# A relational graph layer on one core: ScalarE's order within a block, stores in four pieces, a bank for the totals, dense comparisons

## What is computed

```
h = relu(layernorm(x))                                   # (6250, 128)
dots   = sum((h[src] @ tokeys.T) * relations[rel] * (h[src] @ toqueries.T), axis=1) / 128
values = exp(dots)
fr     = src + 6250 * rel
values = values / segment_sum(values, fr)[fr]
output = segment_sum(values[:, None] * h[dst], fr)       # (16 * 6250, 128)
weights = einsum('rb,bij->rij', comps, bases_w)          # 16 matrices of 128 x 128
out = relu(einsum('rij,rnj->ni', weights, output))
return x + out
```

## Time and profile before

| | |
|---|---|
| median of 3 runs | 2487.49 us (2487.05 to 2491.51) |
| profiled execution, its own time | 2487.54 us |
| its span, first to last instruction | 2485.8 us (1.7 us lie around it) |
| PE busy | 1327.6 us, 53% of the span |
| DVE busy | 1336.7 us, 54% |
| ACT busy | 454.1 us, 18% |
| POOL busy | 1613.0 us, 65% |
| mean granted TensorE clock | 0.723 |

### The profile page before, as it was taken

How to read it: one execution, slowest core, us unless ns; L and a number is a source line. 1 busy time by engine, 2 the same in 40 slices (tenths; PEclk the granted TensorE clock), 3 DMA queues, 4 the chain that set the end, 5 groups by cost and what they waited for, 6 DMA issues and landing times.

```text
span 2485.8 us, 30053 instructions
## 1 busy us (share of the span) xinstructions
PE 1327.6 (53%) x9063; PEld 1000.5 (40%) x9113; DVE 1336.7 (54%) x2311; ACT 454.1 (18%) x868; POOL 1613.0 (65%) x1828
## 2 busy tenths in 40 slices
PE   2888988345453535454454545463545454454443
PEld 2665666234242424334342434342434344343433
DVE  7888888474545454454545454545454444545450
ACT  3555555210101011111101010101011111111010
POOL 3122222377777777777777777777777777777775
PEclk8999999666666767676666666666767676666666
DMA  4333333122222222222222222222222222222222
GB/s 124 139 139 127 134 139 137 53 54 56 54 56 54 55 54 56 54 55 54 56 55 54 56 54 56 54 56 54 56 54 56 54 56 54 55 54 56 55 54 41
DMA packets 77959, 170.30 MB, mean 69 GB/s; under 512 B 29796, under 2 KB 45148, under 8 KB 71511
## 3 DMA queue, kind: packets, MB, share of 16 engines
q0 software_dynamic: 52576, 106.12, 17.1%
q1 hardware_dynamic: 25010, 63.79, 7.0%
q10 hardware_dynamic: 352, 0.14, 0.0%
HBM read 112.99 MB, written 57.82 MB: 69 GB/s over the span
## 4 chain that ended last, share of the span: by engine, by line
POOL 59%; issue 21%; PE 15%; DMA 2%; DVE 1%; POOLq 1%; ACT 1%; SPq 0%; ACTq 0%; DVEq 0%
POOL arena L456 59%; PE bank L1112 7%; PE bank L1097 3%; PE bank L1065 1%; ACT H L907 1%; POOLq L448 1%; DMA bucket_streams<-REC,IDXW 1%; PE bank L1087 1%; PE bank L1104 1%; PE bank L1078 0%; DMA stage<-in_edge_type 0%; PE bank L1105 0%; PE bank L1225 0%; DVE stats L555 0%; PE bank L1123 0%
## 5 line engine op out<-in xcount | busy, mean ns | idle before, releaser
L456 POOL DMA_INDIRECT arena<-Z_messages,IDX x1593 | 1504.0, 944 | 495.3 <-issue 485.1
L1225 PE MATMUL bank<-arena 128*128 128x128 f32 x3528 | 514.7, 320 | 747.0 <-DMA arena<-Z_messages,IDX 747.0
L1225 PEld LDWEIGHTS bank<-arena 128*128 128x128 f32 x3528 | 506.8, 235 | 757.3 <-issue 757.3
L763 DVE SCALAR_TENSOR_TENSOR O<-bank,X 128x128 f32<-128x128 f32 x49 | 14.3, 292 | 725.4 <-PE bank L1225 725.4
L1015 ACT COPY pay_all<-bank 128x1024 bf16<-128x1024 bf16 x147 | 108.0, 807 | 1368.1 <-PE bank L1192 1359.5
L755 DVE TENSOR_TENSOR arena<-stage,bank 128x512 f32<-128x512 bf16 x441 | 267.7, 678 | 0.2 <-PE bank L1213 0.2
L419 POOL DMA_INDIRECT bucket_streams<-REC,IDXW x50 | 52.1, 1042 | 310.8 <-ACT REC L950 296.9
L698 DVE TENSOR_TENSOR stage<-bank,NLF 128x4608 bf16<-128x4608 f32 x49 | 242.4, 4947 | 0.0
L1182 PE MATMUL bank<-stage,OHR 128*128 128x512 bf16 (+1 forms) x392 | 181.4, 626 | 36.0 <-DVE arena L755 25.7
L1213 PE MATMUL bank<-pay_all 128*128 128x256 bf16 x882 | 136.5, 284 | 114.5 <-DVE arena L755 109.7
L1112 PE MATMUL bank<-WT,HT 128*128 128x512 f32 x392 | 186.9, 617 | 0.0
(11 more groups left out here) (177 smaller groups left out, 1465.2 us busy)
## 6 DMA issues: line engine op xcount, KB each, us to landing
Z_messages<-stage SPq DMA_DIRECT2D x48, 1024.0 KB, 3.9
arena<-Z_messages,IDX POOLq DMA_INDIRECT x1593
X<-in_x SPq DMA_DIRECT2D x4, 768.0 KB, 13.0
out<-O SPq DMA_DIRECT2D x48, 64.0 KB
arena<-in_L_gnn_bases_w SPq DMA_DIRECT2D x1, 1024.0 KB, 15.3
bucket_streams<-arena SPq DMA_DIRECT2D x1, 882.0 KB
bucket_streams<-bucket_streams SPq DMA_DIRECT2D x49, 18.0 KB
RL<-bucket_streams SPq DMA_DIRECT2D x49, 18.0 KB
```

The costliest lines, as they stand in the source:

```text
L456: g.indirect_dma_start(Gbuf[par][:, k, :], None, Z, bass.IndirectOffsetOnAxis(IDX[par][:, k:k + 1], 0))\
L1225: mm = t_.matmul(bank[2][:, 0:EMB], OW[:, k, :], Gbuf[par][:, k, :], start=(k == 0), stop=(k == G - 1))
```

## The change

- `normalise(i + 1)` moves on ACT from behind the fourth message copy to between the second and the third. `copy_z` gets bounds for that.
- `store_z` issues four transfers of 512 columns, each as soon as its copy is done, in place of one of 2048. The semaphore totals of the stores go from 16 to 64 a block wherever they are waited for.
- ACT makes a dense copy `q1` of the bucket column. `LOC` and the shifted comparisons work on single values in place of doubled ones. `ranks` reads `LOC` as a broadcast.
- The totals go to bank 7 in place of bank 3. The matmul of L1150 runs before step 51 in place of after it, and the totals wait for the last chunk count and no longer for the last record copies. Those waits stand behind them.

```diff
-        LOC2 = sb("LOC2", [EP, NCOL, 2], F16)
+        LOC = sb("LOC", [EP, NCOL], F16)
+        q1 = sb("q1", [EP, NCOL], F16)
...
             def store_z(i, par, skip, n=P):
-                sp.wait_ge(s["z_sb"], i * 4 + 4)
                 zr = Z[bass.ds(i * (P * R) + skip * R, n * R), :].rearrange("(p r) i -> p (r i)", r=R)
-                sp.dma_start(zr, ZS[par][0:n, :]).then_inc(zst[par], 16)
+                for k in range(4):
+                    sp.wait_ge(s["z_sb"], i * 4 + k + 1)
+                    sp.dma_start(zr[:, k * 512:(k + 1) * 512], ZS[par][0:n, k * 512:(k + 1) * 512]).then_inc(zst[par], 16)
...
-            by_group = lambda ap: ap.rearrange("p (g j) two -> p g j two", j=GW)
-            q_group, local = by_group(q2[:]), by_group(LOC2[:])
-            v.memset(local[:, :, 0, :], 0.0).then_inc(s["loc"], 1)
-            v.tensor_tensor(local[:, :, 1:GW, :], q_group[:, :, 1:GW, :], q_group[:, :, 0:GW - 1, :], ALU.is_equal)\
+            by_group = lambda ap: ap.rearrange("p (g j) -> p g j", j=GW)
+            q_group, local = by_group(q1[:]), by_group(LOC[:])
+            dve.wait_ge(s["dense"], 1)
+            v.memset(local[:, :, 0], 0.0).then_inc(s["loc"], 1)
+            v.tensor_tensor(local[:, :, 1:GW], q_group[:, :, 1:GW], q_group[:, :, 0:GW - 1], ALU.is_equal)\
                 .then_inc(s["loc"], 1)
...
-                    v.tensor_tensor(equal_at(d), q_group[:, :, d:GW, :], q_group[:, :, 0:GW - d, :], ALU.is_equal)\
+                    v.tensor_tensor(equal_at(d), q_group[:, :, d:GW], q_group[:, :, 0:GW - d], ALU.is_equal)\
                         .then_inc(s["loc"], 1)
...
-                    v.tensor_tensor(local[:, :, d - 1:GW, :], local[:, :, d - 1:GW, :], equal_at(d - 1), ALU.add)\
+                    v.tensor_tensor(local[:, :, d - 1:GW], local[:, :, d - 1:GW], equal_at(d - 1), ALU.add)\
                         .then_inc(s["loc"], 1)
...
-                v.tensor_tensor(RK2[:], RK16[:].unsqueeze(2).broadcast_to([EP, TC, 2]), LOC2[:, bass.ds(i * TC, TC), :],
+                v.tensor_tensor(RK2[:], RK16[:].unsqueeze(2).broadcast_to([EP, TC, 2]), LOC[:, bass.ds(i * TC, TC)].unsqueeze(2).broadcast_to([EP, TC, 2]),
                                 ALU.add).then_inc(s["rk"], 1)
...
-            v.tensor_copy(ROWI[:], bank[3][0:1, 0:4 * NB + 1]).then_inc(s["nt_row"], 1)
+            v.tensor_copy(ROWI[:], bank[7][0:1, 0:4 * NB + 1]).then_inc(s["nt_row"], 1)
...
                 for c in range(2):
                     a.activation(half[:, :, c], whole, ACT.Copy, bias=low).then_inc(s["dup"], 1)
+                if k == 0:
+                    a.activation(q1[:], whole, ACT.Copy).then_inc(s["dense"], 1)
...
                     copy_so(i)
-                    copy_z(i, par)
+                    copy_z(i, par, 0, 2)
                 if dyn(i) or i + 1 < NB:
                     normalise(i + 1)
+                if dyn(i) or i < NB:
+                    copy_z(i, par, 2, 4)
                 if dyn(i) or 2 <= i:
                     copy_rec(i - 2, par)
...
-            run_steps(pe, step, NCH + 1)
+            run_steps(pe, step, NCH)
             pe.wait_ge(s["s8_sb"], NCH)
             pe.wait_ge(s["ends"], 2)
             t_.matmul(bank[0][0:NB, 0:2], both[:], ENDS[:], start=True, stop=True).then_inc(s["ends_mm"], 1)
+            step(NCH + 1, (NCH + 1) % 2)
+            pe.wait_ge(s["ncount"], NCH)
...
             pe.wait_ge(s["rec_sb"], NCH)
             pe.wait_ge(s["v"], NCH)
```

More of the change, by code:

```diff
@@ L144, in program @@
         own8 = late[:, G // 2 * P + 2 * P:G // 2 * P + 2 * P + 16 * P].bitcast(F32).rearrange("p (t n) -> p t n", t=8)
-        same = [pay_all[0:EP, p, 0:2 * NCOL // GW * (GW - 1)] for p in range(2)]
+        same = [pay_all[0:EP, p, 0:NCOL // GW * (GW - 1)] for p in range(2)]
         DS = [sb(f"DS{p}", [WIN, 2 * NS], F16) for p in range(2)]
@@ L206, in program @@
         names = """const x_in0 x_in1 x_in2 x_in3 x_in4 w_in bases_in edges_in kq_t kq_sb wt_mm wt_sb comps_d edge edges_done
-            dup loc stat varr stdd ln ohb s8 s8_sb bt bt_sb ncount own fold half m_sum rk ohs idxw mx pos pay d_mm d_sb rec_mm rec_sb scat
+            dup dense loc stat varr stdd ln ohb s8 s8_sb bt bt_sb ncount own fold half m_sum rk ohs idxw mx pos pay d_mm d_sb rec_mm rec_sb scat
             h th ht so_mm so_sb prod z_mm z_sb zst0 zst1 zrow v ends ends_mm nt nt_mm nt_row join sp_go marks_sb marks_st
@@ L338, in _ @@
             with sp.If(bad > 0):
-                sp.wait_ge(zst[0], 16 * ((NB + 1) // 2))
-                sp.wait_ge(zst[1], 16 * (NB // 2))
+                sp.wait_ge(zst[0], 64 * ((NB + 1) // 2))
+                sp.wait_ge(zst[1], 64 * (NB // 2))
                 for k, a in enumerate((src, dst, rel)):
@@ L438, in _ @@
             run_steps(pool, step, NCH + 1)
-            pool.wait_ge(zst[0], 16 * ((NB + 1) // 2))
-            pool.wait_ge(zst[1], 16 * (NB // 2))
+            pool.wait_ge(zst[0], 64 * ((NB + 1) // 2))
+            pool.wait_ge(zst[1], 64 * (NB // 2))
             pool.wait_ge(s["zrow"], 16)
@@ L530, in _ @@
             bucket_onehot(0, 0)
-            by_group = lambda ap: ap.rearrange("p (g j) two -> p g j two", j=GW)
-            q_group, local = by_group(q2[:]), by_group(LOC2[:])
-            v.memset(local[:, :, 0, :], 0.0).then_inc(s["loc"], 1)
-            v.tensor_tensor(local[:, :, 1:GW, :], q_group[:, :, 1:GW, :], q_group[:, :, 0:GW - 1, :], ALU.is_equal)\
+            by_group = lambda ap: ap.rearrange("p (g j) -> p g j", j=GW)
[3 more added lines that the diff above has]
+            v.tensor_tensor(local[:, :, 1:GW], q_group[:, :, 1:GW], q_group[:, :, 0:GW - 1], ALU.is_equal)\
                 .then_inc(s["loc"], 1)
             def equal_at(d):
-                return same[d % 2][:, 0:2 * NCOL // GW * (GW - d)].rearrange("p (g j two) -> p g j two", j=GW - d, two=2)
+                return same[d % 2][:, 0:NCOL // GW * (GW - d)].rearrange("p (g j) -> p g j", j=GW - d)
             for d in range(2, GW + 1):
@@ L785, in _ @@
                 for p in range(2):
-                    dve.wait_ge(zst[p], 16 * ((NB + 1 - p) // 2))
+                    dve.wait_ge(zst[p], 64 * ((NB + 1 - p) // 2))
                 v.tensor_copy(iotaP, iotaN[:]).then_inc(s["iota_p"], 1)
@@ L955, in copy_rec, with copy_z @@
                     a.copy(stats[0:1, 0, 0:1], stats[0:1, 0, 1:2]).then_inc(s["v"], 1)
-            def copy_z(i, par):
-                for k in range(4):
+            def copy_z(i, par, lo, hi):
+                for k in range(lo, hi):
                     act.wait_ge(s["z_mm"], i * 4 + k + 1)
@@ L990, in _ @@
             for i in range(4):
-                step(i, i % 2, (i // 2) * 16)
+                step(i, i % 2, (i // 2) * 64)
             with act.Fori(2, (NB - 1) // 2) as j:
-                step(j * 2, 0, j * 16)
-                step(j * 2 + 1, 1, j * 16)
+                step(j * 2, 0, j * 64)
+                step(j * 2 + 1, 1, j * 64)
             for i in range(NB - 1, NCH + 2):
-                step(i, i % 2, (i // 2) * 16)
+                step(i, i % 2, (i // 2) * 64)
             act.wait_ge(s["nt_row"], 1)
@@ L1150, in _ @@
             t_.matmul(bank[0][0:NB, 0:2], both[:], ENDS[:], start=True, stop=True).then_inc(s["ends_mm"], 1)
+            step(NCH + 1, (NCH + 1) % 2)
+            pe.wait_ge(s["ncount"], NCH)
+            pe.wait_ge(s["nt"], 10)
+            t_.transpose(bank[7][0:1, 3 * NB + 1:4 * NB + 1], POS[0:NB, NCH:NCH + 1], identf[0:NB, 0:NB])
+            t_.matmul(bank[7][0:1, 0:NB], NT[:, 1:2], identf[0:NB, 0:NB], start=True, stop=True)
+            for p in range(2):
+                t_.matmul(bank[7][0:1, (1 + p) * NB:(2 + p) * NB], NT[:, 2 + p:3 + p], upto16[:], start=True, stop=True)
+            t_.matmul(bank[7][0:1, 3 * NB:3 * NB + 1], NT[:, 4:5], upto16[:, NB - 1:NB], start=True, stop=True)\
+                .then_inc(s["nt_mm"], 1)
+            pe.wait_ge(s["nt_row"], 1)
             pe.wait_ge(s["rec_sb"], NCH)
             pe.wait_ge(s["v"], NCH)
[L1154 to L1161, removed]
             bad = pe.value_load(ROWI[0:1, 3 * NB:3 * NB + 1], min_val=0, max_val=16 * NB)
```

## The result

| | before | after |
|---|---|---|
| median | 2487.27 us (4 runs, 2486.23 to 2491.51) | 2431.19 us (4 runs, 2430.80 to 2433.53) |
| profiled execution: own time, span | 2487.54, 2485.8 us | 2430.94, 2429.2 us |
| ratio after to before | | 0.9773, 95% interval 0.9756 to 0.9790 |

The forecast was 2436.5 us, range 2429 to 2450. The change gained 56.1 us where 51.0 were forecast, and the time lies inside the range, 2.2 us above its lower end. Lines move: L1087 of before is L1094 after, L907 is L912, L962 is L967, L1125 is L1132, L419 is L421, L456 is L458.

What follows compares the result with a forecast made beforehand. TensorE, nearest to full, was taken to bound the block loop with a hole waiting for H, and POOL's gathers the unchanged 2007 us bucket phase. 43.2 + 4.3 + 0 + 3.5 = 51.0 off 2487.5 gave 2436.5 us, range 2429 to 2450.

Steps and rivals of the forecast that it cites:

- The sum: Whole kernel: 43.2 + 4.3 + 0 + 3.5 = 51.0 us off 2487.5, giving 2436.5 us.
- Which stretch: Bucket phase stays at 2007 us, all gain in the first 479; over 3 us difference there means wrong.
- H moved: Block loop: TensorE's transpose no longer waits for H; 0.90 us a block, 43.2 us in all, ends 39.8 and 47.2.
- Rival B: Block loop: a chain through ACT's copy and DVE holds the period above TensorE's floor; 2458 us, chance 0.10.
- Rival C: Block loop: moving H frees nothing, as the transpose finds another late input; 2480 us, chance 0.03.
- Stores in pieces, in the loop: Block loop: 1 MB in 2 KB rows takes 2.7 to 3.6 us a period, hidden; cost 0.
- Rival D: Block loop: stores bound it if 2 KB rows hold engines 0.34 us each; 2612 us, chance 0.03.
- Dense comparisons: Setup on DVE: half the values save 5.1 us, less 0.8 for odd offsets and short rows; 4.3 us.
- Rival A: Setup: dense comparisons lose DVE's paired rate and save nothing; 2440.8 us, chance 0.15.
- Totals: Totals in bank 7: ROWI comes about 6 us earlier but was hidden by 5 us; gain 0.
- Stores in pieces, at the end: Last scatters: those beside the last store land in 4.0 us, not 6.6; last landing 3.5 us earlier.
- rival E: End of the totals: last scatters get slower because the store lasts longer, 4.1 us lost; 2444.1 us, chance 0.08.

Runs made afterwards that it cites:

- by_offset: Changed kernel with ACT's dense copy stored by place within the group, so each comparison and addition runs over one contiguous stretch at an even offset; 2428.70 us.
- late_pieces: Changed kernel with the four pieces of each store all issued after the fourth message copy; 2434.86 us.
- dense_only: Kernel before with only the dense comparisons (extra ACT copy, LOC on single values, ranks on a broadcast); 2485.07 us, ratio 0.9992.
- h_only: Kernel before with only H of the next block moved between the second and third message copy; 2435.73 us, ratio 0.9794.
- stores_only: Kernel before with only the stores issued in four pieces, each after its copy; 2485.14 us, ratio 0.9993.
- h_first: Changed kernel with H ahead of the first message copy in place of between the second and third; 2435.67 us.
- totals_only: Kernel before with only the totals moved to bank 7; 2487.47 us, ratio 1.0001.
- tail_split: Changed kernel with the last block's stores issued as 96 rows and 10 rows in place of 106; 2424.22 us.
- both: Changed kernel with the last stores in 96 and 10 rows and the dense copy stored by place within the group; 2422.79 us.
- both_bank3: Changed kernel with last stores in 96 and 10 rows, dense copy by place in the group, and totals in bank 3 as before; 2423.05 us.

## Why the prediction was right, step by step

**The sum.** It came out as near as it did in part by luck. Over 48 blocks the move of `H` gave 51.1 us where 43.2 were forecast (49.9 in the periods and 1.2 in block 0, see below). The comparisons brought block 0 forward by 2.7 us where 4.3 were forecast, and the scatters gave 1.2 for 3.5. Another 1.3 us came from an earlier rise of TensorE's clock, for which the forecast had nothing. The miss of `H` by 7.9 us and that of the other two terms by 3.9 go opposite ways.

**Which stretch.** Right: the bucket phase moved by 0.20 us of 2007, and all of the gain came ahead of it. The sign that I gave, more than 3 us of difference there, was set too tight: the twelve profiled executions have 2006.4 to 2011.3 us there for the same work.

**H moved: right in mechanism, too small.** 43.2 us forecast for 48 blocks. Measured: 49.9 for 47 periods, 1.06 each, where my ends were 0.83 and 0.98, and a period of 6.97 where I gave 7.09 to 7.20. The term that was mis-sized is the one that took the gain from TensorE's counted idle time and stopped at 0.90. From start to start the hole went from 1.04 to 0.05 in the mean over the loop, so 1.00: I had the 1.05 of one block before me and took 0.1 off it for an ordinary distance, while its neighbours stand 0.05 apart. The rest, about 0.07, lies just behind the hole. In means over the loop, transpose to sums went from 0.19 to 0.14 and sums to compaction from 0.71 to 0.69, perhaps because weights can now load under the matmul before; that was not tried. Rival B, a chain through DVE that holds the period, did not come: DVE is at 312.06 / 47 = 6.64 us of 6.97, and TensorE itself is full. Rival C, that the move frees nothing, is out by the same 49.9 us. H alone settles that this edit is the cause.

**Stores in pieces, in the loop: right.** Cost 0. The DMA share over the 47 periods is 0.42, so a block's store takes at most 0.42 x 6.97 = 2.9 us of all engines (scatters included), at the lower end of the 2.7 to 3.6 given. Rival D is off by a factor of four: at most 2.9 x 16 / 512 = 0.09 us a row, where it had 0.34 and needed 0.25. The 10 us a block for pieces one behind the other did not come either; besides, "DMA: Bandwidth & Descriptors" of the Trainium skill gives the 2 us, in its section on the anatomy of one DMA, for transfers that GpSimd issues, and SP issues these.

**Dense comparisons: right in kind, 4.3 forecast, 2.9 measured** (the chain from 12.09 to 9.19 us). Rival A, that all is lost, is out: the comparison of 1000 values read from an odd offset takes 0.77 us, not the 1.2 that one value a cycle would take, and 0.67 in one stretch. On reading, then, the alignment that "VectorE: DVE Perf Modes" of the Trainium skill asks for did not cost the paired rate, and "Vector Engine (DVE) Microarchitecture Reference" of the Trainium skill, section 5.1, has it nearly right. Nearly, because its pair that spans two rows does not show: comparisons in 200 rows of 5, 3 and 1 values take 0.77, 0.58 and 0.52 us, within 0.02 us of those in rows of 6, 4 and 2 (0.76, 0.58, 0.52), as if each row were one value longer. On writing, the sign that I gave came out between: 1400 values took 1.26 us, where 0.9 was the forecast's and 1.6 rival A's, and the statistics began at 35.36 and not at 34. The term I mis-sized is the 0.8 us for odd offsets and short rows: rows written at odd offsets cost 0.38, 0.58 and 0.79 us in three additions alone and 0.44 in the first comparison, which no row before showed. `by_offset` shows it by taking it away, together with the short rows.

**Totals: right,** 0 forecast and 0 measured. The row is copied at 401.02, and DVE then waits for the stores to 409.92, the last scatter landing at 413.4:

```profile
401.02 0.35 DVE L664 CAST ROWI<-bank 1x197 int32<-1x197 f32 x1 [0.83 <-PE bank L1166]
409.92 0.29 DVE L791 CAST bank<-iotaN 128x128 f32<-128x128 bf16 x1 [8.55 <-DMA Z_messages<-stage]
```

**Stores in pieces, at the end: right in sign, 3.5 forecast, 1.2 measured.** The chain of after answers to the earlier trace rows (start, us):

```profile
393.68 5.46 DMA bucket_streams<-REC,IDXW
...
400.12 5.61 DMA bucket_streams<-REC,IDXW
...
406.70 3.41 DMA bucket_streams<-REC,IDXW
...
411.09 2.30 DMA bucket_streams<-REC,IDXW
...
422.36 0.99 POOL arena L458
```

I took 4.0 us a landing, from a count by rows (3.6) and one by bytes (6.6). It is 5.46 and 5.61, and the third scatter is held as well (3.41), because the store now lasts to 409.6. So rival E was half there: one scatter got slower, by 0.85 us, against 1.15 and 1.01 us less in the first two. Both counts were about row size, and `late_pieces` shows that it matters little (6.2 to 6.5 against 6.6). What helped was the early start, most likely because a part of the store was already done. What exactly of the store's work a scatter waits for on those two engines stays open.

**What the forecast didn't have: block 0.** It went from 9.49 to 6.94 us. Part of the 2.55 is the same hole as in the other blocks. The rest is TensorE's clock, which rises from 1.2 to 2.4 GHz at another moment. Windows of before, then of after (us; PE busy; clock; DMA share; GB/s):

```profile
52.00:56.00 4.00, 3.13 (x19) 0.50 0.00 0
56.00:59.00 3.00, 3.00 (x7) 0.50 0.00 0
59.00:60.00 1.00, 1.00 (x3) 0.78 0.00 0
60.00:62.00 2.00, 1.62 (x4) 1.00 0.00 0
```

```profile
49.00:54.00 5.00, 4.13 (x23) 0.50 0.00 0
54.00:55.00 1.00, 1.00 (x3) 0.97 0.00 0
55.00:57.00 2.00, 2.00 (x6) 1.00 0.20 76
```

In both TensorE was nearly idle until just before the loop (at most 0.85 us busy of the 15 us from 35 to 50), and then got busy. Over all kernels, this is when the clock rose, counted from the transpose of block 0, and how long block 0 took (us):

| without the move of `H` | rise | block 0 | with it | rise | block 0 |
|---|---|---|---|---|---|
| before | 6.25 | 9.49 | after | 3.62 | 6.94 |
| `dense_only` | 4.15 | 8.45 | `h_only` | 4.52 | 7.40 |
| `stores_only` | 3.11 | 7.93 | `h_first` | 3.43 | 6.86 |
| `totals_only` | 3.93 | 8.34 | `late_pieces` | 4.53 | 7.40 |
| | | | `tail_split` | 6.16 | 8.21 |
| | | | `by_offset` | 5.32 | 7.80 |
| | | | `both` | 5.19 | 7.73 |
| | | | `both_bank3` | 3.52 | 6.90 |

On the left block 0 is 6.37 us plus half of the time to the rise, on the right 5.14 us plus half of it, each within 0.01: what is done before the rise goes at half the rate. So the 2.55 us are 1.23 for the move of `H` and 1.3 for the clock. Within each group block 0 differs by up to 1.6 us with the moment of the rise, and a gain of 2 us measured elsewhere can hide behind that. That the clock rose earlier in the profiled execution of after is not shown to be an effect of the change: with the earlier setup it rose anywhere from 3.4 to 6.2 us, and without it from 3.1 to 6.3.

## What to carry to other kernels

Where an engine waits once a block for a short instruction of another, look at what stands ahead of that instruction in its queue, and put it into an idle gap between two that have no hurry; price it from start to start of the waiting engine's instructions, less the distance its neighbours keep, not from its counted idle time. Here that gives 1.00 of the 1.06 us measured, the idle time 0.83. Look for a long transfer that occupies only a few engines while others wait behind it; issuing the last 106 rows as 96 and 10 gained 7.0 us here. When a 16-bit vector operation is cut to half its data, look at how its written rows come to lie: half the values saved 2.9 us of 5.1 with rows at odd offsets, and 5.5 once each operation was one stretch.

## What the runs showed of the hardware that I had not expected

- 16-bit additions on DVE that write rows at an odd offset took 1.05 us for 200 rows whatever their length (5, 3 or 1 values), against 0.77, 0.57 and 0.52 us for rows of 6, 4 and 2 at even ones. The 1000, 600 and 200 values in one stretch took 0.67, 0.47 and 0.26 us.
- POOL's small operations got slower in the changed loop: the cast to `IDXW` (L408 before, 0.19 us) and the product (L427 before, 0.48 us) after, busy us and mean ns:

```profile
L410 POOL CAST IDXW<-POS 100x1 int32 (+1 forms) x46 | 44.4, 965 | 0.0
L429 POOL TENSOR_TENSOR PR<-SO 128x128 f32<-128x128 f32 x46 | 41.7, 907 | 6.7 <-ACT SO L941 5.3
```

  The move of `H` brings it (0.94 and 0.90 us in `h_only`, 0.19 and 0.48 in `stores_only`). In the changed loop the cast falls beside DVE's product of 125x1600: 200.65 to 201.67 us, against 200.64 to 201.63; before, DVE was idle at that place. It cost nothing here, POOL being idle for more than half of the period. That DVE's operation causes it was not tried.
- A scatter took 6.6 us beside a store that kept two engines busy, 3.0 beside one of 128 rows, with a share of 0.77 of all sixteen, and 2.3 beside none.
- ACT's copy of 1600 values from 32-bit to 16-bit took 7.1 us when it wrote with a stride of 200 values, and 1.5 densely.
